# Where a query norm is multiplied in, and which engine forms the gate products, in a local-attention kernel on one core

## The chip, the cores and the metric

One Trainium2 chip, one core. The metric is the device time of one execution in microseconds, lower is better. The kernel before takes 1637.84 us, the median of three runs (1637.82 to 1640.18).

## The reference, cut to what matters

The input `x` is 16 sequences of 512 tokens with 128 features. The result is `x + _L0_attn_ref(xn) + _L0_ffn_ref(xn)` with `xn` the layer norm of `x`. The first is an attention among the 16 heads of each token, the second two layers of a local-attention block (`_layer`). The change touches only the layers, 16 sequences times 2 layers, called 32 units below. Per unit:

```python
q, k, v = to_heads(q), to_heads(k), to_heads(v)     # 8 heads of 64
q = l2norm(q) * qs
k = l2norm(k) * ksc
q, k = rotary_xpos(q, k)
sim = einsum('bhwid,bhwjd->bhwij', bq * QK_SCALE, bk)   # windows of 64, each sees itself and the one before
attn = softmax(where(mask, -max, sim))
...
h = layernorm(shift_token(x)) @ w1 + b1
a, g = split(h, 2)                                   # 341 wide each
x = x + (a * gelu(g)) @ w2 + b2
```

The rotation is linear, so the division by the norm of q may come before it, after it, or as a factor of the scores: softmax(rn * s) needs rn * s and the maximum times rn.

## The kernel before

**Units and blocks.** A unit (sequence s, layer l) has four blocks of 128 tokens. Every piece of work is a step (kind, s, l, n); a table gives each kind a slot (`UNIT_SLOTS` and the like, lines 50 to 95), `all_steps` (L123) adds the unit's place times `PERIOD` and sorts all steps by that number. Each engine's program walks this one sorted list and issues its own kinds in that order, so the slots alone set the order of every queue: TensorE, VectorE, ScalarE, GpSimd, and SyncE, which issues all transfers of the loop. The slots are no times; only their order acts. Semaphores (`Signal`, L171) make each step wait for what it reads and for the buffer that it overwrites. Five PSUM banks go round as a ring (`Ring`, L199): whichever is released earliest in the list is taken next, and `released_by` (L190) names the step that gives a bank back.

**One unit, as far as it matters here.** Per block: TensorE projects q and k (`project_qk`), ScalarE squares them (`square`, L621), VectorE multiplies by the rotary tables (`rope`, L808 and L813) and sums the squares (`ssq`, L823). GpSimd adds the two rotary parts over 1024 columns (`rope_add`, L554), and for two blocks at a time works out 1/norm of all 16 heads in twelve small operations (`rnorm`, L562, its lines in `newton` L515 to L530), into `rn`. Its step `normed` (L567) multiplies **k alone**, 512 columns, by its norm. TensorE transposes q and k (`qk_t`, L947), ScalarE copies them out of PSUM (`q_copy`, `k_copy`, line 597 as all plain copies), TensorE forms scores for the block as two half-blocks of four heads, one PSUM bank each (`scores`, L955 the mask and L961). VectorE takes the negated row maxima (`row_max`, L828, into `nmx`), and **GpSimd multiplies them by the norm of q** (`row_scale`, L577, into `nml`). ScalarE takes the exponentials, four ACTIVATEs of 128 columns per half-block, each followed by a read of its accumulator (`exp`, L644):

```python
nc.scalar.activation(pl[:, k, m, :], ps[:, m * P:(m + 1) * P], ACT.Exp, bias=nml[:, k, m:m + 1],
                     scale=rn[:, TURN[step] // 2 % RNS, 2 * m + n % 2:2 * m + n % 2 + 1], accum_out=suml[:, k, m:m + 1])
```

Both `bias` and `scale` are operands with one value per partition, called pointer operands here. That is 32 exponentials per unit, 1024 in all. VectorE forms the reciprocals of the sums (`row_recip`, L833). The probabilities are multiplied by them (`scale`): of the eight half-blocks of a unit, `POOL_SCALED = (1, 4, 6)` are done by GpSimd in one operation of 512 columns (L582), the other five by ScalarE in four of 128 (L651). Then come transposes (`probs_t`, L972), copies (`p_copy`), the products with v (`values`, L983; v was moved by transfers of SyncE, `move_v`, L474), a projection (`out_local`), a residual sum, a layer norm (`norm2`, L667), and the MLP.

**The MLP's gate.** For each of three column tiles (128, 128 and 85 rows of 512 columns) TensorE fills two banks (`up`). ScalarE takes the gelu of one into `gate` (`gelu`, L679, two buffers) and copies the other with its bias into `hid` (`up_copy`, L684). GpSimd multiplies the two (`hid`, L572), and `down` (L1024) waits for the third. ScalarE loads a function table before the first gelu of a unit and another before the next exponential.

Beside the units, the attention among heads (`_L0_attn_ref`) of each sequence runs on GpSimd (`product`, L549, 4.6 us each) and VectorE (L773, L784, L789, 2.3 us each), in single instructions that nothing can interrupt.

Of the kernel before, what the change touches and what calls it, by code (L numbers as in the profile page):

```python
# [13 lines left out]
P = 128  # L14
# [7 lines left out]
HT = 3  # L22
# [8 lines left out]
POOL_SCALED = (1, 4, 6)  # L31
# [10 lines left out]
FIRST_AT = (-1.2708745, 0.6010711, 2.0036151, 3.0013583, 4.0029550)  # L42
LAST_AT = (-5.0039757, -2.9663610, -1.9718764, -0.5737843, 0.4163776)
FIRST_HEADS = (0, 1, 2)
LAST_HEADS = (B - 2, B - 1)
HEADS_AT = (0.3413570, 0.4991559, 3.8117712, -4.4646283, -0.4851747)
HEADS_SCALE = (0.5958681, 1.1193597, 0.7838495, 1.0049087, 1.0274403)
# [9 lines left out]
    "k_copy": (165.0988, 171.4118, 184.9169, 201.8379), "scores": (170.7924, 176.2910, 190.1140, 206.8248),  # L57
    "row_max": (171.0266, 177.1326, 191.8920, 208.8231), "row_scale": (174.5908, 177.7892, 192.9950, 210.0411),
    "exp": (175.3308, 177.3865, 180.4114, 180.8920, 197.7475, 202.1735, 211.3702, 214.1910),
    "row_recip": (176.4316, 179.0744, 180.6813, 185.4614, 201.2478, 206.9631, 215.6879, 217.2619),  # L60
    "scale": (178.1679, 183.5201, 183.8322, 190.7280, 204.5029, 208.7350, 217.6800, 218.5197),
    "probs_t": (186.1063, 189.5048, 192.4912, 194.5274, 207.2222, 216.5516, 221.8074, 222.0460),
    "p_copy": (189.4922, 191.8301, 194.7040, 195.6005, 209.2029, 217.9046, 221.8298, 222.6642),
    "values": (196.4822, 199.5495, 223.8159, 224.0189), "o_copy": (199.8882, 201.3287, 225.0351, 226.7589),
    "out_local": (227.5112,), "x2": (230.4382,), "shift_x2": (233.0435,), "stats2": (235.6252,), "aggr2": (236.6378,),
    "rstd2": (237.6456,), "norm2": (242.9309,), "norm2_t": (244.3596,), "high2": (245.4327,), "low2": (245.7646,),
# [3 lines left out]
FIRST_SLOTS = {  # L70
    "shift_x": (117.3139,), "x1": (269.0942,), "shift_x1": (276.6645,), "x1_t": (276.8388,), "x1_split": (278.5542,),
    "x1_low": (280.0510,),
}
IN_SLOTS = {
    "load": (-60.4848,), "stats": (-40.1689,), "aggr": (-36.5136,), "rstd1": (-20.2682,), "norm": (15.7589,),
    "norm_t": (53.5376,), "x_split": (55.0099,), "x_low": (57.5271,),
}
HEADS_SLOTS = {
    "qkv_full": (78.2153, 89.6956, 104.7573, 110.3161), "qkv_bias": (81.5013, 91.1173, 108.0542, 113.9984),
    "product": (94.5851, 118.2468, 144.2400, 170.3617), "full_scores": (107.8015, 126.3480, 156.7184, 181.3058),  # L80
    "full_max": (109.2799, 132.3223, 160.4979, 185.2952), "full_less": (110.6705, 133.8879, 161.9904, 186.5792),
    "full_exp": (113.5148, 136.6825, 163.8463, 191.2888), "full_values": (116.5251, 143.0822, 166.7757, 194.4942),
    "full_out": (118.8605, 148.3945, 172.8347, 204.0966), "full_norm": (124.1554, 151.7265, 176.7351, 207.5981),
    "heads": (152.8697, 167.4103, 214.8847, 227.9640),
}
OUT_SLOTS = {
    "heads_load": (226.2026,), "attn_t": (237.0812,), "o_t": (241.2655,),
}
PREP_SLOTS = {
    "split_w3": (-91.8590,), "split_q": (65.5914, 68.6233), "tables": (61.3455, 105.5114), "fold": (145.8522,),  # L90
    "gain": (161.8664,), "split_up": (179.3697,), "biases": (148.4283,),
}
LAST_SLOTS = {
    "x_again": (236.0293,), "result": (270.2713,), "add_x": (270.8445,), "store": (329.0087,),
# [128 lines left out]
def build(nc, t, out):  # L223
    with ExitStack() as ctx:
# [43 lines left out]
        nmx = sb("nmx", [P, 4, 4])  # L268
# [85 lines left out]
        s_nml = signal("row_maxima_scaled", "row_scale")  # L354
# [21 lines left out]
        s_hid = signal("hidden", "hid")  # L376
        s_down = signal("down_filled", "down")
# [15 lines left out]
        def hidden_rows(n):  # L393
# [110 lines left out]
        def _(pool):  # L504
# [27 lines left out]
            for step in STEPS:  # L532
# [30 lines left out]
                if kind == "normed":  # L563
                    k3 = qk[:, TURN[step] % QKB, INNER:2 * INNER].rearrange("p (h d) -> p h d", d=LD)
                    pool.wait_ge(s_add.sem, s_add.at(same("rope_add", step, n), step))
                    pool.wait_ge(s_rn.sem, s_rn.at(same("rnorm", step, n // 2), step))
                    nc.gpsimd.tensor_tensor(k3, k3, rn[:, TURN[step] % RNS, LH:2 * LH, None].to_broadcast([P, LH, LD]), ALU.mult).then_inc(s_nrm.sem, 1)  # L567
                if kind == "hid":
                    pool.wait_ge(s_upc.sem, s_upc.at(same("up_copy", step, n), step))
                    pool.wait_ge(s_gelu.sem, s_gelu.at(same("gelu", step, n), step))  # L570
                    rows = hidden_rows(n)
                    nc.gpsimd.tensor_tensor(hid[rows, n, :], hid[rows, n, :], gate[rows, TURN[step] % 2, :], ALU.mult).then_inc(s_hid.sem, 1)  # L572
                if kind == "row_scale":
                    k = 2 * TURN[step] % PLS
                    pool.wait_ge(s_max.sem, s_max.at(same("row_max", step, n), step))
                    in_order(same("normed", step, n), step)
                    nc.gpsimd.tensor_tensor(nml[:, k:k + 2, :], nmx[:, 2 * TURN[step] % 4:2 * TURN[step] % 4 + 2, :],  # L577
# [513 lines left out]
```

## Time and profile before

| | |
|---|---|
| median of the runs | 1637.84 us |
| the profiled execution's own time | 1640.42 us |
| its span, from the first to the last instruction | 1638.6 us |
| mean granted TensorE clock | 0.969 of full speed |
| instructions | 40224 |
| function-table loads on ScalarE | 64 |

The profile is one execution. Busy time of an engine is the time covered by at least one of its instructions; ScalarE and GpSimd issue the next instruction before the last one's record has ended, so a mean duration is longer than what the instruction costs in a full queue. That cost is read from the distance between starts in the timeline.

### The profile page before, as it was taken

To read this page: it belongs to the slowest core of one execution; us is meant where nothing else is said; L and a number is where in the kernel's file an instruction comes from. 1 tells how busy PE (TensorE), PEld (TensorE's weight loads), DVE (VectorE), ACT (ScalarE), POOL (GpSimd) and SP (SyncE) were. 2 spreads that over 40 slices of the span, in tenths; PEclk is the share of its full clock that TensorE was granted. 3 is DMA by queue.
4 is the path that set the end of the run, shared out by engine and by line. 5 is a ranking of instruction groups with operands and counts; after the bars stand their busy time and mean duration, and the time that the engine had idled before them with its cause. 6 is when DMAs were issued, how large, how long until landed. Compare 5 with 4: busy or idle time off the path is not lost.

```text
span 1638.6 us, 40224 instructions
## 1 busy us (share of the span) xinstructions
PE 1384.8 (85%) x14680; PEld 1099.8 (67%) x14680; DVE 1342.5 (82%) x2149; ACT 1472.9 (90%) x4176; POOL 1237.4 (76%) x1607
## 2 busy tenths in 40 slices
PE   1578789998989989898989989998998988688885
PEld 1366577777777767777777767777777776577664
DVE  4998899898989989898888989898888686558731
ACT  1468799999999999999999999999999999598993
POOL 2758788787888888888888888788878784577741
PEclk9788899999999999999999999999999999899998
DMA  5021012221211122221211122121211211111120
GB/s 153 10 42 39 11 35 48 47 46 36 59 34 40 31 48 47 41 51 32 60 34 37 33 48 47 41 47 35 61 32 34 39 40 39 19 27 34 22 54 21
DMA packets 177637, 67.82 MB, mean 41 GB/s; under 512 B 146933, under 2 KB 152354, under 8 KB 177442
## 3 DMA queue, kind: packets, MB, share of 16 engines
q1 hardware_dynamic: 176146, 64.70, 18.7%
q8 instruction: 118, 1.93, 0.5%
q14 instruction: 77, 0.63, 0.1%
q10 hardware_dynamic: 1296, 0.56, 0.1%
HBM read 17.54 MB, written 8.39 MB: 16 GB/s over the span
## 4 chain that ended last, share of the span: by engine, by line
ACT 70%; PE 10%; issue 9%; DVE 5%; POOL 3%; DMA 1%; SPq 1%; ACTq 0%; DVEq 0%; POOLq 0%
ACT sb_pl L644 24%; ACT sb_pl L651 10%; ACT sb_pT L597 5%; ACT sb_sq L621 4%; ACT sb_kT L597 3%; ACT sb_oTl L597 3%; ACT sb_hid L684 3%; ACT sb_v L597 3%; ACT sb_hn L667 3%; ACT sb_qT L597 3%; PE banks L983 2%; ACT L679 2%; ACT L644 2%; ACT sb_gate L679 2%; PE banks L972 2%
## 5 line engine op out<-in xcount | busy, mean ns | idle before, releaser
L644 ACT ACTIVATE sb_pl<-banks,sb_nml,sb_rn 128x128 f32<-128x128 f32 x1024 | 466.0, 515 | 5.2 <-POOL sb_nml L577 4.8
L554 POOL TENSOR_TENSOR sb_qk<-sb_qk,sb_t 128x1024 f32<-128x1024 f32 x128 | 304.8, 2381 | 47.4 <-DVE sb_t L813 47.4
L549 POOL TENSOR_TENSOR sb_pr<-sb_qkvf 128x2048 f32<-128x2048 f32 x64 | 291.8, 4559 | 3.7 <-DVE sb_qkvf L767 3.7
L644 ACT ACTIVATION_READ_ACCUMULATOR sb_pl<-banks,sb_nml,sb_rn 128x1 f32 x1024 | 268.7, 262 | 0.0
L651 ACT ACTIVATE sb_pl<-sb_pl,sb_rl 128x128 f32<-128x128 f32 x640 | 213.1, 459 | 0.2 <-DVE sb_rl L833 0.2
L883 PE MATMUL banks<-sb_wqh,sb_hh 128*128 128x512 f32 x384 | 175.7, 458 | 43.6 <-DVE sb_t L813 34.5
L828 DVE TENSOR_REDUCE sb_nmx<-banks 128x4 f32<-128x512 f32 x256 | 164.1, 683 | 42.2 <-PE banks L961 42.1
L972 PE MATMUL banks<-sb_ident,sb_pl 128*128 128x128 f32 x1024 | 162.3, 283 | 27.7 <-ACT sb_kT L597 10.5
L621 ACT ACTIVATE sb_sq<-banks 128x1024 f32<-128x1024 f32 x128 | 137.3, 1073 | 44.1 <-PE banks L885 44.1
L597 ACT ACTIVATE sb_pT<-banks 128x512 f32<-128x512 f32 x256 | 165.8, 672 | 4.6 <-PE banks L972 4.5
L808 DVE TENSOR_TENSOR sb_qk<-banks,sb_tab 128x1024 f32<-128x1024 f32 x128 | 154.9, 1210 | 12.7 <-ACT sb_sq L621 12.6
L813 DVE TENSOR_TENSOR sb_t<-banks,sb_tab 128x512 f32<-128x512 f32 x256 | 163.5, 680 | 0.0
L572 POOL TENSOR_TENSOR sb_hid<-sb_hid,sb_gate 128x512 f32<-128x512 f32 (+1 forms) x96 | 122.5, 1285 | 53.9 <-ACT sb_hid L684 45.0
L972 PEld LDWEIGHTS banks<-sb_ident,sb_pl 128*128 128x128 f32 x1024 | 118.5, 143 | 64.1 <-issue 17.2
L947 PE MATMUL banks<-sb_ident,sb_qk 128*128 128x128 f32 x1024 | 146.3, 284 | 15.9 <-POOL sb_qk L567 11.7
L884 PE MATMUL banks<-sb_wql,sb_hh 128*128 128x512 f32 x384 | 157.5, 410 | 0.0
L885 PE MATMUL banks<-sb_wqh,sb_hl 128*128 128x512 f32 x384 | 157.5, 410 | 0.0
L823 DVE TENSOR_REDUCE sb_ssq<-sb_sq 128x16 f32<-128x1024 f32 x128 | 154.4, 1206 | 3.2 <-ACT sb_sq L621 3.2
L784 DVE TENSOR_TENSOR sb_pr<-banks,sb_qkvf 128x2048 f32<-128x2048 f32 x64 | 146.1, 2282 | 2.2
L961 PE MATMUL banks<-sb_kT,sb_qT 64*64 64x128 f32 x4096 | 144.5, 279 | 3.8 <-ACT sb_kT L597 3.8
L773 DVE TENSOR_REDUCE banks<-sb_pr 128x256 f32<-128x2048 f32 x64 | 145.8, 2279 | 0.0
L789 DVE TENSOR_REDUCE banks<-sb_pr 128x128 f32<-128x2048 f32 x64 | 145.6, 2275 | 0.0
(120 smaller groups left out, 3698.2 us busy)
## 6 DMA issues: line engine op xcount, KB each, us to landing
sb_vs<-sb_v SPq DMA_DIRECT2D x224, 128.0 KB, 2.4
sb_xt<-x SPq DMA_DIRECT2D x16, 256.0 KB, 3.0
heads_scratch<-sb_ofs SPq DMA_DIRECT2D x64, 64.0 KB, 3.3
sb_orow<-heads_scratch SPq DMA_DIRECT2D x16, 256.0 KB, 2.9
sb_ob<-x SPq DMA_DIRECT2D x16, 256.0 KB, 2.9
out<-sb_ob SPq DMA_DIRECT2D x16, 256.0 KB, 3.4
sb_hh<-sb_sh SPq DMA_DIRECT2D x16, 128.0 KB, 2.4
sb_hl<-sb_sl SPq DMA_DIRECT2D x16, 128.0 KB, 2.4
```

What stands on the lines that cost most here:

```text
L549: nc.gpsimd.tensor_tensor(pr[:].rearrange("p (q k d) -> p q k d", q=H, k=H), q[:, :, None, :].to_broadcast([P, H, H, D]), k[:, None, :, :] ...
L554: nc.gpsimd.tensor_tensor(qk[:, k, :], qk[:, k, :], t2[:, TURN[step] % 2, :], ALU.add).then_inc(s_add.sem, 1)
L597: return nc.scalar.activation(dst, src, ACT.Copy)
L621: nc.scalar.activation(sq[:, TURN[step] % 2, :], qk_ps, ACT.Square).then_inc(s_sq.sem, 1)
L644: last = nc.scalar.activation(pl[:, k, m, :], ps[:, m * P:(m + 1) * P], ACT.Exp, bias=nml[:, k, m:m + 1], scale=rn[:, TURN[step] // 2 % RN ...
L651: last = nc.scalar.activation(pl[:, k, m, :], pl[:, k, m, :], ACT.Copy, scale=rl[:, k, m:m + 1])
L813: last = nc.vector.tensor_tensor(t4[:, :, :, dst], q4[:, :, :, src], tab[:, l, n, 1, :, None, src].to_broadcast([P, 2, LH, 32]), ALU.mult)
L828: nc.vector.tensor_reduce(nmx[:, k + h, :], bank(same("scores", step, n), h).rearrange("p (a b) -> p a b", a=4), AX_X, ALU.max, negate=Tru ...
L883: mm(dst, ah, bh, start=True, stop=False)
L884: mm(dst, ah, bl, start=False, stop=False)
L885: return mm(dst, al, bh, start=False, stop=True)
L972: last = nc.tensor.transpose(ps[:, k * P:(k + 1) * P], pl[:, TURN[step] % PLS, k, :], ident[:])
```

## The change

It does five things.

1. `normed` on GpSimd multiplies q and k, 1024 columns, by their norms. The exponentials no longer have a `scale` operand and keep `bias`. `row_scale` is gone (128 operations); VectorE writes the negated maxima into `nml` itself, and `exp` waits for the maximum of its own half-block instead of the scaled maxima of both.
2. `POOL_HID = 1`: the first two gate products of a unit move to VectorE as one `scalar_tensor_tensor` that reads the PSUM bank, adds the bias and multiplies by the gate. Their two `up_copy` steps on ScalarE are gone. The third tile keeps `up_copy` and its product on GpSimd (`pool_hid`). `down` waits for both.
3. The banks of the first two tiles are released by `hid` on VectorE, no longer by `up_copy`. `gelu` waits for the product two before it, on whichever engine.
4. `POOL_SCALED = (2, 6)`: half-blocks 1 and 4 go to ScalarE and 2 to GpSimd, so ScalarE scales six and GpSimd two.
5. All slots are new, so every queue has a new order. The number of steps of other kinds is unchanged.

```diff
-POOL_SCALED = (1, 4, 6)
+POOL_HID = 1
+POOL_SCALED = (2, 6)
...
-    "normed": (154.4511, 162.8918, 182.9419, 183.7601), "project_v": (159.0725, 181.4664, 186.1013, 186.6209),
+    "normed": (182.3337, 183.2623, 200.1915, 201.2225), "project_v": (200.5275, 202.4083, 204.4952, 210.4119),
-    "v_copy": (159.9898, 183.8122, 188.2271, 189.9351), "move_v": (168.5510, 184.9583, 202.4625, 215.3760),
+    "v_copy": (201.3236, 202.6291, 210.9356, 212.3257), "move_v": (209.6570, 215.0451, 216.1022, 229.2302),
-    "qk_t": (161.6890, 171.0966, 184.0998, 201.0989), "q_copy": (164.6524, 171.1983, 185.3925, 201.7627),
+    "qk_t": (187.2993, 188.4284, 207.6851, 212.1740), "q_copy": (187.3831, 189.7285, 211.3468, 213.2392),
-    "values": (196.4822, 199.5495, 223.8159, 224.0189), "o_copy": (199.8882, 201.3287, 225.0351, 226.7589),
+    "values": (220.1959, 226.6013, 244.7089, 245.8630), "o_copy": (222.9003, 228.4260, 245.1633, 246.9817),
-    "up": (252.0156, 253.3813, 259.6720), "gelu": (252.2978, 256.7997, 260.5403), "up_copy": (253.6282, 256.7797, 260.7344),
-    "hid": (255.5584, 258.3963, 261.1113), "down": (266.3925,),
+    "up": (270.6924, 273.5245, 275.3137), "gelu": (273.1911, 273.8595, 275.4467), "up_copy": (276.3338,),
+    "hid": (275.1511, 275.2248), "pool_hid": (281.9469,), "down": (285.2914,),
...
-            "up": ("gelu", "up_copy")[k], "down": ("x1", "add_x")[l], "attn_t": "o_t"}[kind]
+            "up": ("gelu", "hid" if n < HT - POOL_HID else "up_copy")[k], "down": ("x1", "add_x")[l], "attn_t": "o_t"}[kind]
+    if last == "up_copy":
+        n -= HT - POOL_HID
...
+        def gated(step):
+
+            part = step[3] - (HT - POOL_HID)
+            return (s_hid, same("hid", step, step[3])) if part < 0 else (s_phid, same("pool_hid", step, part))
...
                 if kind == "normed":
-                    k3 = qk[:, TURN[step] % QKB, INNER:2 * INNER].rearrange("p (h d) -> p h d", d=LD)
+                    both = qk[:, TURN[step] % QKB, :].rearrange("p (h d) -> p h d", d=LD)
...
-                    nc.gpsimd.tensor_tensor(k3, k3, rn[:, TURN[step] % RNS, LH:2 * LH, None].to_broadcast([P, LH, LD]), ALU.mult).then_inc(s_nrm.sem, 1)
-                if kind == "hid":
+                    nc.gpsimd.tensor_tensor(both, both, rn[:, TURN[step] % RNS, :, None].to_broadcast([P, 2 * LH, LD]), ALU.mult).then_inc(s_nrm.sem, 1)
+                if kind == "pool_hid":
...
-                if kind == "row_scale":
...
-                    act.wait_ge(s_nml.sem, s_nml.at(same("row_scale", step, n // 2), step))
+                    act.wait_ge(s_max.sem, s_max.at(same("row_max", step, n // 2), step, n % 2 + 1))
...
                         last = nc.scalar.activation(pl[:, k, m, :], ps[:, m * P:(m + 1) * P], ACT.Exp, bias=nml[:, k, m:m + 1],
-                                                    scale=rn[:, TURN[step] // 2 % RNS, 2 * m + n % 2:2 * m + n % 2 + 1], accum_out=suml[:, k, m:m + 1])
+                                                    accum_out=suml[:, k, m:m + 1])
...
                     if before(step, 2):
-                        act.wait_ge(s_hid.sem, s_hid.at(("hid", *before(step, 2)[1:]), step))
+                        done, last = gated(before(step, 2))
+                        act.wait_ge(done.sem, done.at(last, step))
...
+                if kind == "hid":
+                    dve.wait_ge(s_up.sem, s_up.at(same("up", step, n), step, 2))
+                    dve.wait_ge(s_gelu.sem, s_gelu.at(same("gelu", step, n), step))
+                    rows, gates = hidden_rows(n), gate[hidden_rows(n), TURN[same("gelu", step, n)] % 2, :]
+                    nc.vector.scalar_tensor_tensor(hid[rows, n, :], bank(same("up", step, n), 1)[rows, :], b1[rows, l, 0, n:n + 1], gates,
+                                                   ALU.add, ALU.mult).then_inc(s_hid.sem, 1)
...
-                    pe.wait_ge(s_hid.sem, s_hid.at(same("hid", step, HT - 1), step))
+                    pe.wait_ge(s_hid.sem, s_hid.at(same("hid", step, HT - POOL_HID - 1), step))
+                    pe.wait_ge(s_phid.sem, s_phid.at(same("pool_hid", step, POOL_HID - 1), step))
```

## Rows read from the trace of the kernel before

**Rows 1.** The page, part 1: busy us (share of the span) xinstructions of each engine.

```profile
PE 1384.8 (85%) x14680; PEld 1099.8 (67%) x14680; DVE 1342.5 (82%) x2149; ACT 1472.9 (90%) x4176; POOL 1237.4 (76%) x1607
```

**Rows 2.** Busy time by stretch: length, PE, PEld, DVE, ACT, POOL, granted clock, DMA share, GB/s.

```profile
200.00:300.00 100.00, 88.58 (x931) 71.35 (x932) 91.63 (x147) 96.51 (x280) 83.98 (x103) 0.97 0.19 39
300.00:1300.00 1000.00, 909.56 (x9901) 721.00 (x9900) 887.18 (x1430) 990.35 (x2816) 832.01 (x1079) 1.00 0.21 43
1300.00:1639.00 339.00, 267.90 (x2815) 214.77 (x2815) 203.75 (x335) 277.11 (x780) 198.74 (x274) 0.94 0.14 31
```

**Rows 3.** Busy time by stretch, ACT's instructions of line 644 alone.

```profile
300.00:1300.00 1000.00, 356.62 (x1398) 1.00 0.21 43
```

**Rows 4.** Timeline of ACT, 700 to 748 us: start us, us, engine line op, shapes xcount.

```profile
702.53 0.46 ACT L644 ACTIVATE sb_pl<-banks,sb_nml,sb_rn 128x128 f32<-128x128 f32 x1
702.87 0.20 ACT L644 ACTIVATION_READ_ACCUMULATOR sb_pl<-banks,sb_nml,sb_rn 128x1 f32 x1
702.97 0.46 ACT L644 ACTIVATE sb_pl<-banks,sb_nml,sb_rn 128x128 f32<-128x128 f32 x1
...
712.11 1.35 ACT L651 ACTIVATE sb_pl<-sb_pl,sb_rl 128x128 f32<-128x128 f32 x4
713.28 1.09 ACT L621 ACTIVATE sb_sq<-banks 128x1024 f32<-128x1024 f32 x1
714.19 0.67 ACT L597 ACTIVATE sb_kT<-banks 128x512 f32<-128x512 f32 x1
714.66 0.68 ACT L597 ACTIVATE sb_qT<-banks 128x512 f32<-128x512 f32 x1
...
719.00 1.76 ACT L667 ACTIVATE sb_hn<-sb_x,sb_nmr,sb_rs 128x128 f32<-128x128 f32 x4
720.53 1.14 ACT L621 ACTIVATE sb_sq<-banks 128x1024 f32<-128x1024 f32 x1
...
728.62 1.28 ACT L679 ACT_TABLE_LOAD   x1
...
730.51 1.26 ACT L684 ACTIVATE sb_hid<-banks,sb_b 128x512 f32<-128x512 f32 x2
731.65 0.70 ACT L679 ACTIVATE sb_gate<-banks,sb_b 128x512 f32<-128x512 f32 x1
```

**Rows 5.** Groups by line and shape, ACT: xcount | busy us, mean ns | idle before.

```profile
L644 ACT ACTIVATE sb_pl<-banks,sb_nml,sb_rn 128x128 f32<-128x128 f32 x1024 | 466.0, 515 | 5.2 <-POOL sb_nml L577 4.8
L684 ACT ACTIVATE sb_hid<-banks,sb_b 128x512 f32<-128x512 f32 x64 | 42.4, 687 | 2.0 <-PE banks L885 2.0
```

**Rows 6.** The same view, POOL.

```profile
L554 POOL TENSOR_TENSOR sb_qk<-sb_qk,sb_t 128x1024 f32<-128x1024 f32 x128 | 304.8, 2381 | 47.4 <-DVE sb_t L813 47.4
...
L567 POOL TENSOR_TENSOR sb_qk<-sb_qk,sb_rn 128x512 f32<-128x512 f32 x128 | 133.8, 1046 | 4.4 <-issue 0.2
L582 POOL TENSOR_TENSOR sb_pl<-sb_pl,sb_rl 128x512 f32<-128x512 f32 x96 | 100.0, 1042 | 18.7 <-DVE sb_rl L833 18.7
L572 POOL TENSOR_TENSOR sb_hid<-sb_hid,sb_gate 128x512 f32<-128x512 f32 x64 | 81.5, 1284 | 38.9 <-ACT sb_hid L684 31.1 <-ACT sb_gate L679 7.8
...
L577 POOL TENSOR_TENSOR sb_nml<-sb_nmx,sb_rn 128x8 f32<-128x8 f32 x128 | 26.4, 207 | 59.6 <-DVE sb_nmx L828 59.4
```

**Rows 7.** The same view, DVE.

```profile
L857 DVE TENSOR_TENSOR sb_ml<-banks,sb_mh 128x512 fp32r<-128x512 f32 x32 | 22.1, 690 | 21.0 <-ACT sb_mh L597 20.8
```

**Rows 8.** Waits: engine, tile, line <- releaser: us in total, times, longest us.

```profile
DVE sb_rl L833 <- ACT sb_pl L644: 114.2, 103, 5.5
...
POOL sb_hid L572 <- ACT sb_hid L684: 45.0, 43, 8.1
...
POOL sb_hid L572 <- ACT sb_gate L679: 7.8, 14, 1.3
```

**Rows 9.** Waits of SyncE's own queue.

```profile
SPq L474 <- ACT sb_v L597: 452.8, 94, 26.1
```

**Rows 10.** The page, part 6: issues of transfers, KB each, us to landing.

```profile
sb_vs<-sb_v SPq DMA_DIRECT2D x224, 128.0 KB, 2.4
```

More of the change, by code:

```diff
@@ new lines @@
+    "k_copy": (188.2736, 192.0604, 211.5250, 213.9970), "scores": (191.0638, 195.0615, 213.0631, 225.7847),
+    "row_max": (191.4764, 195.6861, 216.0966, 226.7308),
+    "exp": (194.8833, 195.1833, 198.4961, 199.0827, 217.7930, 219.3748, 232.3456, 234.6785),
+    "row_recip": (195.2384, 196.7062, 202.6297, 203.8389, 222.8514, 225.3115, 237.9346, 238.1178),
+    "scale": (198.4786, 200.7005, 204.5438, 205.6352, 225.1242, 227.7413, 240.0089, 241.5326),
+    "probs_t": (201.3321, 205.9735, 214.4449, 214.6785, 228.5205, 239.9675, 241.9608, 243.5301),
@@ L69 @@
+    "hid": (275.1511, 275.2248), "pool_hid": (281.9469,), "down": (285.2914,),
 }
 FIRST_SLOTS = {
-    "shift_x": (117.3139,), "x1": (269.0942,), "shift_x1": (276.6645,), "x1_t": (276.8388,), "x1_split": (278.5542,),
-    "x1_low": (280.0510,),
+    "shift_x": (140.0838,), "x1": (286.1484,), "shift_x1": (286.2087,), "x1_t": (292.8402,), "x1_split": (294.2011,),
+    "x1_low": (294.7821,),
 }
 IN_SLOTS = {
-    "load": (-60.4848,), "stats": (-40.1689,), "aggr": (-36.5136,), "rstd1": (-20.2682,), "norm": (15.7589,),
@@ L76 @@
-    "norm_t": (53.5376,), "x_split": (55.0099,), "x_low": (57.5271,),
+    "load": (-43.2744,), "stats": (-42.8030,), "aggr": (-36.2465,), "rstd1": (-6.3194,), "norm": (27.1315,),
+    "norm_t": (75.6752,), "x_split": (77.7525,), "x_low": (79.2937,),
 }
 HEADS_SLOTS = {
-    "qkv_full": (78.2153, 89.6956, 104.7573, 110.3161), "qkv_bias": (81.5013, 91.1173, 108.0542, 113.9984),
-    "product": (94.5851, 118.2468, 144.2400, 170.3617), "full_scores": (107.8015, 126.3480, 156.7184, 181.3058),
-    "full_max": (109.2799, 132.3223, 160.4979, 185.2952), "full_less": (110.6705, 133.8879, 161.9904, 186.5792),
@@ L563, in _ @@
                 if kind == "normed":
-                    k3 = qk[:, TURN[step] % QKB, INNER:2 * INNER].rearrange("p (h d) -> p h d", d=LD)
+                    both = qk[:, TURN[step] % QKB, :].rearrange("p (h d) -> p h d", d=LD)
                     pool.wait_ge(s_add.sem, s_add.at(same("rope_add", step, n), step))
                     pool.wait_ge(s_rn.sem, s_rn.at(same("rnorm", step, n // 2), step))
-                    nc.gpsimd.tensor_tensor(k3, k3, rn[:, TURN[step] % RNS, LH:2 * LH, None].to_broadcast([P, LH, LD]), ALU.mult).then_inc(s_nrm.sem, 1)
-                if kind == "hid":
+                    nc.gpsimd.tensor_tensor(both, both, rn[:, TURN[step] % RNS, :, None].to_broadcast([P, 2 * LH, LD]), ALU.mult).then_inc(s_nrm.sem, 1)
+                if kind == "pool_hid":
+                    part = HT - POOL_HID + n
                     pool.wait_ge(s_upc.sem, s_upc.at(same("up_copy", step, n), step))
-                    pool.wait_ge(s_gelu.sem, s_gelu.at(same("gelu", step, n), step))
-                    rows = hidden_rows(n)
-                    nc.gpsimd.tensor_tensor(hid[rows, n, :], hid[rows, n, :], gate[rows, TURN[step] % 2, :], ALU.mult).then_inc(s_hid.sem, 1)
-                if kind == "row_scale":
[L574 to L577, printed above, removed]
-                                            rn[:, TURN[step] % RNS, 0:LH].rearrange("p (a h) -> p h a", h=2), ALU.mult).then_inc(s_nml.sem, 1)
+                    pool.wait_ge(s_gelu.sem, s_gelu.at(same("gelu", step, part), step))
+                    rows = hidden_rows(part)
+                    gates = gate[rows, TURN[same("gelu", step, part)] % 2, :]
+                    nc.gpsimd.tensor_tensor(hid[rows, part, :], hid[rows, part, :], gates, ALU.mult).then_inc(s_phid.sem, 1)
                 if kind == "scale" and n in POOL_SCALED:
@@ L680, in _ @@
                 if kind == "up_copy":
-                    act.wait_ge(s_up.sem, s_up.at(same("up", step, n), step, 2))
+                    part = HT - POOL_HID + n
+                    act.wait_ge(s_up.sem, s_up.at(same("up", step, part), step, 2))
                     in_order(same("gelu", step, 0), step)
-                    rows = hidden_rows(n)
-                    nc.scalar.activation(hid[rows, n, :], bank(same("up", step, n), 1)[rows, :], ACT.Identity, bias=b1[rows, l, 0, n:n + 1]).then_inc(s_upc.sem, 1)
+                    rows = hidden_rows(part)
+                    nc.scalar.activation(hid[rows, part, :], bank(same("up", step, part), 1)[rows, :], ACT.Identity, bias=b1[rows, l, 0, part:part + 1]).then_inc(s_upc.sem, 1)
                 if kind == "x1_split":
@@ L819, in _ @@
                     if old:
-                        in_order(same("row_recip", old, 2 * old[3] + 1), step)
+                        in_order(same("row_max", old, old[3]), step)
                         dve.wait_ge(s_rn.sem, s_rn.at(same("rnorm", old, old[3] // 2), step, 1))
```

52 lines of the change are left out of this document (24 added, 28 removed).

## The prediction

> **What bounds the kernel now.** I read the page's shares first: ScalarE is busy 90% of the span, TensorE 85%, VectorE 82% [rows 1]. That is an average, so the busy time by stretch comes next [rows 2]. From 300 to 1300 us, ScalarE is busy 990 of 1000 us, TensorE 910, VectorE 887, GpSimd 832. What limits this stage is ScalarE, and the others wait for it: VectorE's reciprocals wait 114.2 us in all for exponentials [rows 8]. ScalarE itself waits almost never; for the maxima that GpSimd scaled, 4.8 us in all [rows 5].
>
> How long is one unit there? Line 644 has 1398 instructions in that stretch [rows 3]; some 22 are table loads, one per unit, and a unit has 64 others (32 exponentials, 32 accumulator reads), so 1376/64 = 21.5 units, **46.5 us each**. Divided by 21.5, the busy times of a unit are ScalarE 46.1, TensorE 42.3, VectorE 41.3, GpSimd 38.7. ScalarE has 0.4 us of air, the next engine 4.2. TensorE's figure includes matmuls that overlap or wait with modelled ends, so its work is at most that.
>
> **ScalarE, term by term.** Its records overlap, so I price by distances between starts [rows 4].
> - *The scale operand.* A plain copy of 512 columns from PSUM has no pointer operand: 714.19 to 714.66, 0.47 us. The copy with a bias, same shape: 730.51 to 731.65 for two, 0.57 each. One pointer costs 0.10. From SBUF, four scalings with one pointer take 712.11 to 713.28, 0.2925 each; four norms with two pointers 719.00 to 720.53, 0.3825 each: 0.09. An exponential runs 702.53 to its accumulator read at 702.87, and 0.10 later the next one starts, 0.44 in all. I take **0.093 us** for the operand that goes, so 32 x 0.093 = 2.98 us less per unit, 95 us in the run. Bounds: 0.10 above; nothing below, if the read of the accumulator sets the distance. Against the low end: 0.47 less 384 columns at the rate that the square shows (1024 columns in 714.19 - 713.28 = 0.91, so 0.44 for 512 more, 0.33 for 384) leaves 0.14 for 128 columns without pointers; two pointers make 0.33, and 0.34 is seen. The operands explain the whole distance.
> - *Two bias copies fewer*: 2 x 0.57 = -1.14. *One more half-block to scale*: 4 x 0.2925 = +1.17. Together nothing. The third copy stays, and the order still has one block of gelus per unit between exponentials, so 64 table loads as before.
> - Sum: 46.1 - 2.95 = **43.1 us per unit**.
>
> **VectorE.** The gate product reads one PSUM bank and one SBUF tile of 512 columns; the nearest row is such an operation at 0.69 us [rows 7]. Two per unit: +1.38, so 41.3 becomes **42.7**. The added per-partition bias has no row on this engine; below, nothing; above, a second pass, 1.38 for each and 44.1 per unit. I take 0.69, since on ScalarE a pointer costs 0.1 and not a pass. `row_max` writes to another tile, at no cost.
>
> **GpSimd.** `normed` doubles from 512 columns at 1.046 us. Two full inputs go from 1.284 at 512 (line 572) to 2.381 at 1024 (line 554), so 0.19 is fixed; 2 x 1.046 - 0.19 = 1.90. I take 1.90 and keep 2.38 as the upper bound, that of two full inputs: +3.4 (at most +5.3) for four blocks. Gone are four `row_scale` (4 x 0.207), two gate products (2 x 1.284) and one scaling (1.042), 4.4 together [rows 6]. Net -1.0 (at most +0.9): 37.7 to 39.6 per unit, the slackest engine still. The row's 1.90 is 1.86 ns per column. The Trainium skill, GPSIMD Engine Reference, section 3.1, gives about 2.6 cycles an element for two inputs and 4497 ns for 2048, and says to do such products on VectorE; by an estimate from it, 1024 columns take 2.2 us, `normed` adds 4.8 us a unit, and GpSimd comes to 39.1. It advises against this part of the change; by its price, too, GpSimd would not bind.
>
> **The moved waits.** `exp` now waits for VectorE directly. GpSimd stood 59.4 us before `row_scale` [rows 6], a wait with `rope_add` and the long product queued behind it, which goes; what is late next there is the rotary product of VectorE (47.4 us before line 554 [rows 6]). New is a wait on VectorE: `hid` waits for `up` and a gelu, with rotary products and maxima queued behind it. GpSimd waited 45.0 + 7.8 us for the copies and gelus before 96 products [rows 8], 0.55 each; on VectorE that is 1.1 us per unit. It also holds the `up` bank until VectorE gets there, and a VectorE instruction of 2.3 us can be in front. The q norm now lies before `qk_t`, but the k norm already did and needed the same twelve steps; what is added is 0.86 us per block, and the new order does blocks in pairs, so the first transposes of a pair come up to 1.9 + 2.4 us later. In the loop earlier work covers that; without that cover, in the first and the last unit, it would cost some 4 us each.
>
> **Transfers.** None is added. In SyncE's queue `move_v` moves behind later copies of v; it waited 452.8 us in all for them [rows 9], and lands 2.4 us after issue [rows 10]. In the new order it still stands ahead of the `values` that read it by several steps of each engine. I cost it at nothing; if a landing were exposed, TensorE would stand 2.4 us.
>
> **Sum.** Now ScalarE needs 43.1, VectorE 42.7, TensorE at most 42.3. A ScalarE with 0.4 us of air needs the others to be idle 4 us a unit, which they no longer are. From 200 to 300 us, with VectorE at 92%, ScalarE was busy 96.5% [rows 2]: 3.5% of 43.1 is 1.5 us of air. Between 0.4 and 1.5 I take 1.2: **44.3 us per unit**, 2.2 less. Over 21.5 units that is 47 us. The other 10.5 units hold 10.5 x 2.98 = 31 us of the saving; ScalarE is busy 277 of the last 339 us [rows 2] and the start hangs on other engines, so I take 13. In all -60, from the profiled execution's 1640.4 to 1580.4; that execution is 2.6 above the median of the runs, so **1578 us**.
>
> **The rivals.**
> - *All of it arrives* (0.13). ScalarE keeps its 0.4 us: 1637.8 - 94 = 1544, to 1560 with a weaker start. For it: ScalarE hardly waits for anything now. Against: three engines within 1 us.
> - *VectorE becomes the bound* (0.14). It stood 114.2/32 = 3.6 us per unit before the reciprocals [rows 8]. If 1.5 to 2.7 of this stays beside 1.1 of new waits, a unit takes 42.7 + 2.6 to 3.8 = 45.3 to 46.5, and little is left: 1605 to 1634.
> - *The operand is free* (0.08): the accumulator read sets the distance. Then ScalarE stays at 46.1 and VectorE is fuller: 1636 to 1650, half of it within 0.2%. Against it stands the sum of pointers above.
> - *Slower by the gate products* (0.07): VectorE stands at `hid` behind a table load (1.28 us) and a gelu (0.70) [rows 4] with the exponentials ahead. It decides at 46.5 - 42.7 = 3.8 us of new standing per unit, 1.9 for each product. At 2.5 each, a unit takes 47.7: 1.2 x 32 = 38 us more, **1676**. For it: both products are queued together right behind the first gelus. Against it: the 0.55 seen on GpSimd.
> - *The forecast* (0.58): 1562 to 1605.
>
> **The numbers.** A measurement of this kernel tells some 0.2%, 3.3 us, from no change. Faster: 0.58 + 0.13 + 0.14 = 0.85. Same: half the free operand and the edge of VectorE's case, 0.05. Slower: 0.10. The range holds the forecast's own and parts of the two on either side, 1550 to 1618; 2 in 10 stay outside.
>
> **What would show it.** In the profile after: exponential to accumulator read 0.25 instead of 0.34, and 0.35 from one exponential to the next; on ScalarE 64 bias copies fewer and 128 scalings more; `normed` near 1.9 us; the gate product near 0.69 on VectorE; VectorE near 95% busy in the middle, ScalarE 96 to 98%, units 44.3 us apart. The forecast is wrong if the exponential's distance stays, if `hid` on VectorE waits more than 2 us a unit, or if `normed` takes over 2.4.

## The result and the profile after

The changed kernel takes **1541.68 us** (median of 4 runs, 1538.84 to 1544.04) against 1638.24 for the kernel before, ratio 0.9408 with the interval 0.9385 to 0.943. That is 97 us less where I forecast 60, and 8 us below the range. The profiled execution took 1544.04 us, its span is 1542.3.

The page of the changed kernel, part 1, answers to [rows 1]; below it, busy time by stretch answers to [rows 2], in the same columns.

```profile
PE 1355.6 (88%) x14680; PEld 1105.4 (72%) x14680; DVE 1365.6 (89%) x2213; ACT 1378.2 (89%) x4240; POOL 1209.4 (78%) x1383
```

```profile
200.00:300.00 100.00, 89.75 (x941) 72.89 (x940) 89.70 (x142) 93.28 (x289) 82.25 (x87) 0.97 0.20 42
300.00:1300.00 1000.00, 945.48 (x10614) 775.46 (x10613) 958.51 (x1571) 990.09 (x3065) 866.15 (x991) 1.00 0.22 46
```

ScalarE's busy time fell by 94.7 us (1472.9 to 1378.2). In the middle VectorE is busy 959 us of 1000, near the 95% that I had listed; ScalarE is busy 990, as before, where I had listed 96 to 98%.

The operand, in the timeline of ScalarE in the changed kernel (start us, us, engine line op, shapes):

```profile
710.23 0.36 ACT L647 ACTIVATE sb_pl<-banks,sb_nml 128x128 f32<-128x128 f32 x1
710.49 0.20 ACT L647 ACTIVATION_READ_ACCUMULATOR sb_pl<-banks,sb_nml 128x1 f32 x1
710.58 0.37 ACT L647 ACTIVATE sb_pl<-banks,sb_nml 128x128 f32<-128x128 f32 x1
```

From the exponential to its accumulator read 0.26 us, to the next exponential 0.35, where [rows 4] show 0.34 and 0.44: 0.09 us less. The Trainium skill, ScalarE: Activation LUTs, section What ACT_TABLE_LOAD costs, says that each per-partition pointer operand adds about 93 ns; the trace agrees, also for an exponential with an accumulator (0.09 us).

How long a unit is can be read without counting, from the first instruction of the unit's layer norm (`norm2`, L667 before, L670 after; one start per unit). These are those of the fifth and the 27th unit in the timeline of ScalarE, first of the kernel before, then of the changed one.

```profile
349.13 0.62 ACT L667 ACTIVATE sb_hn<-sb_x,sb_nmr,sb_rs 128x128 f32<-128x128 f32 x1
...
1365.76 0.61 ACT L667 ACTIVATE sb_hn<-sb_x,sb_nmr,sb_rs 128x128 f32<-128x128 f32 x1
```

```profile
346.45 0.70 ACT L670 ACTIVATE sb_hn<-sb_x,sb_nmr,sb_rs 128x128 f32<-128x128 f32 x1
...
1295.07 0.69 ACT L670 ACTIVATE sb_hn<-sb_x,sb_nmr,sb_rs 128x128 f32<-128x128 f32 x1
```

Before: 1016.6/22 = 46.21 us per unit. After: 948.6/22 = **43.12**. So 68 us came from these 22 units, 3 from the start (349.1 to 346.5), and 26 from what lies behind the 27th start (1638.6 - 1365.8 = 272.8 against 247.2). This split, start, unit and end, is used for all runs below.

The stretches between these two starts hold 22 whole units, so busy time divided by 22 is free of cut units. First the kernel before, then the changed one, in the columns of [rows 2]:

```profile
349.13:1365.76 1016.63, 923.22 (x10070) 732.01 (x10068) 895.31 (x1443) 1006.04 (x2870) 840.08 (x1095) 1.00 0.20 42
```

```profile
346.45:1295.07 948.62, 897.76 (x10065) 736.71 (x10061) 909.54 (x1487) 940.10 (x2913) 821.12 (x941) 1.00 0.21 45
```

ScalarE is busy 45.7 us per unit before and 42.7 after, and idle 0.5 and 0.4; VectorE is busy 40.7 and 41.3.

The groups by line and shape of the changed kernel give the other prices (count | busy us, mean ns | idle before).

```profile
L574 POOL TENSOR_TENSOR sb_qk<-sb_qk,sb_rn 128x1024 f32<-128x1024 f32 x128 | 241.2, 1906 | 0.6
L867 DVE SCALAR_TENSOR_TENSOR sb_hid<-banks,sb_b,sb_gate 128x512 f32<-128x512 f32 x64 | 45.2, 746 | 14.9 <-ACT sb_gate L683 9.6 <-PE banks L896 5.3
L838 DVE RECIPROCAL sb_rl<-sb_suml 128x4 f32<-128x4 f32 x256 | 37.8, 166 | 15.5 <-ACT sb_pl L647 14.9
```

`normed` takes 1.906 us, where I took 1.90 (by my estimate from the Trainium skill, GPSIMD Engine Reference, section 3.1, it was 2.2; the measurement decides). The gate product takes 0.71 us by its busy time (45.2/64), where I took 0.69, and VectorE waits 14.9 us in all before them, 0.47 per unit and not 1.1. The wait that could have made VectorE the bound is gone: 114.2 us before the reciprocals [rows 8] became 14.9. Their group in the kernel before:

```profile
L833 DVE RECIPROCAL sb_rl<-sb_suml 128x4 f32<-128x4 f32 x256 | 42.2, 166 | 114.6 <-ACT sb_pl L644 114.2
```

### The profile page after: what moved, and what is told of

The parts are those of the page before. It is cut to its first block, busy times and chain, and to the rows that moved or that the text cites. A ratio compares the mean times of both kernels' runs of the same rounds, so it can differ in the third digit from the quotient of the medians.

```text
span 1542.3 us, 40144 instructions
## 1 busy us (share of the span) xinstructions
PE 1355.6 (88%) x14680; PEld 1105.4 (72%) x14680; DVE 1365.6 (89%) x2213; ACT 1378.2 (89%) x4240; POOL 1209.4 (78%) x1383
## 4 chain that ended last, share of the span: by engine, by line
ACT 54%; DVE 19%; PE 12%; issue 6%; DMA 5%; SPq 2%; POOL 1%; POOLq 0%; ACTq 0%; DVEq 0%
ACT sb_pl L647 16%; ACT sb_pl L654 9%; ACT sb_pT L600 4%; ACT sb_gate L683 3%; ACT sb_sq L624 3%; DMA sb_xt<-x 3%; DVE sb_t L818 3%; DVE banks L794 3%; DMA sb_x<-sb_x 2%; DVE sb_pr L789 2%; DVE banks L778 2%; DVE sb_nml L833 2%; ACT sb_oTl L600 2%; DVE sb_qk L813 2%; ACT L647 2%
## 5 line engine op out<-in xcount | busy, mean ns | idle before, releaser
L647 ACT ACTIVATE sb_pl<-banks,sb_nml 128x128 f32<-128x128 f32 x1024 | 369.3, 429 | 15.3 <-DVE sb_nml L833 14.8
L647 ACT ACTIVATION_READ_ACCUMULATOR sb_pl<-banks,sb_nml 128x1 f32 x1024 | 270.4, 269 | 0.0
L654 ACT ACTIVATE sb_pl<-sb_pl,sb_rl 128x128 f32<-128x128 f32 x768 | 259.8, 480 | 0.3 <-DVE sb_rl L838 0.2
L574 POOL TENSOR_TENSOR sb_qk<-sb_qk,sb_rn 128x1024 f32<-128x1024 f32 x128 | 241.2, 1906 | 0.6
L833 DVE TENSOR_REDUCE sb_nml<-banks 128x4 f32<-128x512 f32 x256 | 163.9, 683 | 18.5 <-PE banks L972 18.5
L624 ACT ACTIVATE sb_sq<-banks 128x1024 f32<-128x1024 f32 x128 | 142.1, 1110 | 37.5 <-PE banks L896 37.4
L983 PE MATMUL banks<-sb_ident,sb_pl 128*128 128x128 f32 x1024 | 155.9, 284 | 20.9 <-ACT sb_pl L654 16.9
L958 PE MATMUL banks<-sb_ident,sb_qk 128*128 128x128 f32 x1024 | 140.0, 281 | 16.4 <-ACT sb_pT L600 9.9
L972 PEld LDWEIGHTS banks<-sb_kT,sb_qT 64*64 64x64 f32 x4096 | 111.4, 133 | 49.7 <-issue 45.1
```

The costliest lines, as they stand in the source:

```text
L574: nc.gpsimd.tensor_tensor(both, both, rn[:, TURN[step] % RNS, :, None].to_broadcast([P, 2 * LH, LD]), ALU.mult).then_inc(s_nrm.sem, 1)
L624: nc.scalar.activation(sq[:, TURN[step] % 2, :], qk_ps, ACT.Square).then_inc(s_sq.sem, 1)
L647: last = nc.scalar.activation(pl[:, k, m, :], ps[:, m * P:(m + 1) * P], ACT.Exp, bias=nml[:, k, m:m + 1], accum_out=suml[:, k, m:m + 1])
L654: last = nc.scalar.activation(pl[:, k, m, :], pl[:, k, m, :], ACT.Copy, scale=rl[:, k, m:m + 1])
L833: nc.vector.tensor_reduce(nml[:, k + h, :], bank(same("scores", step, n), h).rearrange("p (a b) -> p a b", a=4), AX_X, ALU.max, negate=Tru ...
L983: last = nc.tensor.transpose(ps[:, k * P:(k + 1) * P], pl[:, TURN[step] % PLS, k, :], ident[:])
```

## The experiments

Each ratio is to the kernel before, run on the same chip, with its 95% interval. "Against the changed kernel" is the difference of the ratios times 1638 us; the changed kernel itself came out at 0.941 on a second chip (d4).

| run | ratio | against the changed kernel | start, unit, end (us) |
|---|---|---|---|
| kernel before | 1 | +97 | 349, 46.21, 273 |
| changed kernel | 0.9408 (0.9385 to 0.943) | 0 | 346, 43.12, 247 |
| a8 norm alone, old order | 0.9646 (0.9632 to 0.966) | +39 | 347, 44.11, 264 |
| a2 all operations, old order | 0.9657 (0.9643 to 0.9672) | +41 | 345, 44.15, 268 |
| a1 operand back | 0.9871 (0.9853 to 0.9889) | +76 | 356, 45.63, 263 |
| a4 gates back | 0.9684 (0.967 to 0.9699) | +45 | 349, 44.24, 264 |
| a5 VectorE, two more | 0.9516 (0.9501 to 0.953) | +18 | 345, 43.66, 252 |
| a6 ScalarE, two more | 0.9532 (0.9516 to 0.9547) | +20 | 350, 43.74, 250 |
| b1 old order, new last places | 0.9717 (0.9702 to 0.9731) | +51 | 344, 44.10, 278 |
| b2 new order, old last places | 0.9615 (0.9601 to 0.9629) | +34 | 345, 43.17, 280 |
| c1 old order, o_copy moved | 0.9784 (0.977 to 0.9799) | +62 | 345, 44.77, 274 |
| c3 new order, o_copy back | 0.9471 (0.9457 to 0.9486) | +10 | 344, 43.52, 250 |
| a7 third half-block on GpSimd | 0.9378 (0.9359 to 0.9397) | -5 | 347, 42.50, 249 |
| a3 order alone | 1.1509 (1.1481 to 1.1538) | +344 | 394, 54.75, 290 |
| d1, d2 out_local moved | 1.0825, 1.0821 | +232 | 367, 51.3, 276 |

**Is the operand the whole saving?** (a1)

```diff
-                                                    accum_out=suml[:, k, m:m + 1])
+                                                    scale=one[:, m:m + 1], accum_out=suml[:, k, m:m + 1])
```

> The changed kernel, but every exponential has a scale operand again, one value per partition from a tile of ones; order, queues and all other work stay those of the changed kernel. Theory A (the operand is the whole saving: ScalarE's queue sets the time and 0.093 us in each of 1024 exponentials arrives in full): 1542 + 95 = 1637 us, 1630 to 1642. Theory B (my forecast's arithmetic was right on the operand, some 60 us, and the new order gave the other 36): 1542 + 60 = 1602, and under 1620. Exponential to accumulator read 0.34 us in both.

Measured: +76 us, 1620.67 in its own runs. That lies between the two theories' 95 and 60; scaled to the changed kernel's chip it is 1617 us, just inside theory B's bound of 1620. The unit grew by 2.51 of the 2.98 us that were put back. The distance from exponential to read is back at 0.35 (702.02 to 702.37 in its timeline). With the operand in place, the change's order and its other parts still save 21 us.

**The norm part alone, and all operations, in the old order** (a8, a2). The slot tables are those of the kernel before; a8 also keeps three gate products and half-blocks 1, 4 and 6 on GpSimd.

```diff
-POOL_HID = 1
-POOL_SCALED = (2, 6)
+POOL_HID = 3
+POOL_SCALED = (1, 4, 6)
```

> Part 1 alone, in the old order: normed over q and k, no scale operand, no scaling of maxima; all three gate products and half-blocks 1, 4 and 6 stay on GpSimd, whose work rises by 3.4 - 0.8 = 2.6 us per unit to 41.3 by its busy time. Theory A: ScalarE's sum is again 43.1 per unit, and GpSimd's 41.3 overstates its work, so 1542 to 1560 us. Theory B (engines within 2 us of each other disturb one another): 1578 to 1600. If parts 2 and 4 of the change were needed to relieve GpSimd, this run is over 1580.

> The changed kernel's operations in the old order: the slot tables of the kernel before, with the two VectorE products where the first two products stood and the third copy and product where the third stood. Theory A: the order matters little, 1542 to 1555 us. Theory B: without the new order the saving is the 60 of the forecast, 1578, and at least 1565.

Measured: 0.9646 and 0.9657, 58 and 56 us less than before. Theory A falls, theory B holds: **without the new order the saving is nearly the 60 us that I forecast**, and the unit takes 44.11 and 44.15 us where I forecast 44.3. In the old order, parts 2 and 4 bring nothing (a2 against a8, the intervals overlap): GpSimd's load in a8, 928 of 1000 us busy in the middle, is carried as it is. (a8 is just over the 1580 us that was to mean that it is not; a2, where the load is gone, is no faster.) The new order brings 41 us, a2 against the changed kernel: 1.03 us in each of 22 units and 21 us at the end.

```profile
300.00:1300.00 1000.00, 922.83 (x10358) 756.24 (x10358) 917.72 (x1488) 976.26 (x2946) 927.67 (x1038) 1.00 0.21 44
```

This is a8's middle, in the columns of [rows 2]: ScalarE 976 of 1000 us, against 990 in both kernels. The same 22 whole units of a2, and then of a8:

```profile
344.80:1316.10 971.30, 893.87 (x10072) 736.60 (x10070) 915.40 (x1489) 950.36 (x2914) 823.90 (x942) 1.00 0.21 44
```

```profile
346.70:1317.00 970.30, 895.65 (x10068) 733.27 (x10066) 888.54 (x1444) 947.89 (x2870) 899.32 (x1008) 1.00 0.21 44
```

ScalarE is idle 0.95 and 1.02 us per unit there, close to the 1.2 of air that I had put in the sum, and 0.39 in the new order. Of the 1.03 us per unit between a2 and the changed kernel that is 0.56; the other 0.47 is in ScalarE's busy records (43.20 against 42.73), for the same operations.

**The order alone, in the old code** (a3).

> The kernel before with nothing but the new slot tables (scaling of maxima right behind each maximum, bias copies right behind their gelus; GpSimd scales half-blocks 1, 4 and 6 as before). Theory A: 1638 us within 10 us, since ScalarE's work is that of before. Theory B: 1600 to 1620.

Measured: 1.1509, which neither theory allows, and the run doesn't tell them apart. I had put the scaling of the maxima right behind each maximum, and in the new order that is a bad place in GpSimd's queue. The waits of a3 between 300 and 1300 us:

```profile
POOL sb_nml L577 <- DVE sb_nmx L828: 193.3, 61, 7.5
```

GpSimd stood 193 us for maxima, with everything behind it, where it stood 59.4 in the whole run before [rows 6]. The run also differs from the changed kernel by the operand and the bias copies, which cost 76 and 45 us by themselves (a1, a4), and its granted clock in that stretch was 0.92, where it was 1.00 before. So the 344 us are not the price of one wait, and what the new order does with the old code stays open. What the run suggests about the change is that `row_scale` ties GpSimd's queue to TensorE and VectorE, and that the change takes that tie away; no run shows what this is worth.

**How near are the other engines?** (a5, a6, a4). One more VectorE product in front of each gate product, or one more copy of ScalarE in front of `q_copy` 0 and 2, into a tile that nobody reads:

```diff
+                    nc.vector.tensor_tensor(spill[rows, :], bank(same("up", step, n), 1)[rows, :], gates, ALU.mult).then_inc(s_spill.sem, 1)
```

> The changed kernel with each VectorE gate product preceded by one more product of the same two inputs into a tile that nobody reads: 64 more instructions, about 0.6 us each in a full queue, 1.2 us per unit. If VectorE has the 1 to 2 us of air that lies between 41.3 busy and 43.1 per unit: under +10 us. If the engines are so close that each sets the time in turn (the idea behind my 1.2 us of air): +20 to +38. Ratio to before 0.945 against 0.955 to 0.964.

> The changed kernel with two more plain copies of 512 columns per unit on ScalarE, into a tile that nobody reads: 2 x 0.48 = 0.96 us per unit. If ScalarE's queue sets the time in full: +31 us, ratio to before 0.960. If it sets only part of it: +15 or less.

Measured: 1.2 us more work per unit on VectorE cost 18 us in all, 0.54 per unit; 0.96 us more on ScalarE cost 20, 0.62 per unit. VectorE's is below my 20 to 38 and over the 10 of the other case; ScalarE's is short of 31. It is also over the 15 of its other case. So added work on either passes on in part, about half and two thirds: the changed kernel does not follow one engine alone. ScalarE's idle time, read over 22 units as above, rose from 0.39 to 0.86 us per unit with the work on VectorE, and fell to 0.17 with the work on ScalarE (busy 42.80 of 43.66 us, and 43.57 of 43.74). Each kind of work was added in one place only, and the share may hang on the place.

> The changed kernel with part 2 undone: all three tiles are copied by ScalarE and multiplied by GpSimd, in the places where the change has its gelus and products. ScalarE gets 2 x 0.57 = 1.14 us more per unit, GpSimd 2.57 more, VectorE 1.4 less. Theory A' (ScalarE's queue sets the unit in this order): +36 us on the changed kernel, ratio to before 0.963. If waits of the copies on a GpSimd that is fuller count too: up to +60. If VectorE's products had cost the loop anything: less than +30.

Measured: +45 us, in the 36 to 60 that was expected. The unit grew by 1.12 us, about the two bias copies (2 x 0.57), and the end by 17 us. In the new order part 2 pays; GpSimd's two added products were not separated from the copies.

**One wait of the old order, taken out and put back** (c1, c3). In the kernel before, ScalarE's last copy of probabilities is followed by `o_copy` 2, which waits for TensorE's `values`. The waits of ScalarE between 300 and 1300 us, first of the kernel before, then of a2, then of the changed kernel:

```profile
ACT sb_oTl L597 <- PE banks L983: 7.9, 21, 0.4
```

```profile
ACT sb_oTl L600 <- PE banks L994: 8.9, 22, 0.4
```

```profile
ACT sb_pl L647 <- DVE sb_nml L833: 6.0, 11, 0.6
ACT sb_hn L670 <- POOL sb_nmr L595: 1.9, 5, 0.6
```

The first two are once per unit, 0.4 us each by the records, 0.54 by the distances between starts (a record's end overlaps the wait). The new order has exponentials of the next unit in between. c1 moves `o_copy` 2 and 3 so in the old order; c3 puts `o_copy` 2 back ahead of these exponentials in the new one. No other queue changes its order. But the ring of banks goes by the places too: by the kernels' own `Ring`, 102 of TensorE's 1425 bank fills follow another earlier user of their bank in c1 than in a2, and 67 in c3 than in the changed kernel, so TensorE's waits for banks can move as well. This was not separated from the move itself. The edit of c1:

```diff
-    "values": (196.4822, 199.5495, 223.8159, 224.0189), "o_copy": (199.8882, 201.3287, 225.0351, 226.7589),
+    "values": (196.4822, 199.5495, 223.8159, 224.0189), "o_copy": (199.8882, 201.3287, 225.3340, 227.3890),
```

> The kernel of a2_old_order with ScalarE's third and fourth copy of heads out of a unit (o_copy 2 and 3) moved behind the first and second group of four exponentials of the next unit, as the new order has them; every other queue is unchanged. In a2 ScalarE stands some 0.54 us per unit between its last copy of probabilities and o_copy 2, until TensorE has formed the values; in the changed kernel it does not. Theory E (the middle of the old order loses to such stands of ScalarE, one by one): the unit falls from 44.15 to 43.6 us, the time by 14 to 18 us, ratio to before 0.955 to 0.958. Theory F (the stands are symptoms of engines that are all full, and another wait takes its place): under 6 us, ratio 0.962 or more.

> The reverse: the changed kernel with o_copy 2 ahead of the next unit's first exponentials, every other queue unchanged. Theory E: +0.5 us per unit, 14 to 18 us, ratio 0.950 to 0.952. Theory F: under 6 us, ratio 0.944 or less.

Measured: c3 costs 10 us, 0.40 per unit, between the two theories; the wait is back (9.5 us, 23 times). c1 does not save 14 to 18 us; it costs 21, on theory F's side. The waits of c1 in the same stretch, of ScalarE and then of TensorE:

```profile
ACT sb_sq L624 <- PE banks L896: 16.5, 32, 1.0
ACT sb_v L600 <- PE banks L896: 8.4, 10, 0.8
```

```profile
PE banks L1004 <- ACT sb_oTl L600: 16.6, 22, 1.0
```

The wait before `o_copy` is gone from ScalarE. Now TensorE stands before `out_local` (L1004), 16.6 us where a2 has 1.7, since the last copy that it reads comes four exponentials later; and the next unit's projection stands behind it in TensorE's queue, so ScalarE waits for that at `square` (L624), 16.5 us where a2 has 0.2. Nearly the same move is worth 10 us in one order and costs 21 in the other. In the new order the projection stands ahead of `out_local`; that this is the reason is not shown.

**Moving the reader too** (d1, d2).

```diff
-    "out_local": (227.5112,), "x2": (230.4382,), "shift_x2": (233.0435,), "stats2": (235.6252,)
+    "out_local": (233.2800,), "x2": (233.5000,), "shift_x2": (233.6000,), "stats2": (235.6252,)
```

> The kernel of c1_old_order_o_copy (copies of heads out moved behind the next unit's first exponentials, 0.9784) with the step that reads them moved too: out_local stands behind the next unit's project_qk 0 on TensorE, with the residual sum and its shift behind it, as the new order has it; ScalarE's queue is that of c1. In c1 ScalarE no longer stands before o_copy 2 but TensorE stands before out_local, and square 0 waits 0.73 us per unit for the projection queued behind it. Theory G (a stand goes only if every queue that it touches is moved together): the unit falls from 44.77 to 43.5 to 44.0 us, ratio 0.952 to 0.962, below a2's 0.9657. Theory F (the engines are too full for it): a new wait takes its place, 0.9657 or more.

> The kernel of a2_old_order with out_local moved as in d1, and the copies of heads out left where they were. Theory G: within 0.5% of a2, ratio 0.961 to 0.970, since ScalarE still stands 0.54 us before o_copy 2. If the place of out_local alone is what counts: 0.960 or less.

Measured: 1.0825 and 1.0821, some 190 us over a2 and on theory F's side for d1, and the same with and without the move of `o_copy`. So the place of `out_local` was wrong in a way of its own: it came behind `project_qk` 0, which waits for VectorE's rotary products of an earlier block, and VectorE, with little moved in its own queue, waits for `out_local` in turn. Waits of d2 between 300 and 1300 us, of TensorE and of VectorE:

```profile
PE banks L894 <- DVE sb_t L818: 106.7, 50, 3.3
```

```profile
DVE sb_x L846 <- PE banks L1004: 93.9, 20, 6.1
DVE sb_st L851 <- DMA sb_x<-sb_x: 60.8, 20, 3.1
```

VectorE stood 4.7 us in each unit for `out_local`, where a2 has 0.1, and 3.0 for the transfer behind it, where a2 has 1.3. TensorE's standing has a second price here. In d2 it stood 2.9 us, up to 713.72, and the granted clock from 714 to 718 us was 0.57, where it was 1.00 from 710 to 714; the projection's matmuls of 512 columns then started 0.43 us apart instead of 0.23. Over the middle the clock was 0.93 in d1 and d2. How the loss divides between the waits and the clock was not measured. Theory G's numbers did not come; its idea stays open, since these moves brought waits of their own.

**The places of the last units** (b1, b2).

```diff
-LAST_AT = (-5.0039757, -2.9663610, -1.9718764, -0.5737843, 0.4163776)
+LAST_AT = (-4.9945847, -2.9959306, -1.9923118, -0.9899664, 0.0148815)
```

> The kernel of a2_old_order (the change's operations in the old order) with one table of places changed: the last five units stand where the changed kernel has them (LAST_AT; the last two units 1.00 periods apart and 0.4 to 0.6 periods earlier). a2 took 0.9657 of the kernel before, and behind its 27th unit it needed 268 us where the changed kernel needs 247. Theory C (the last units' places make that difference): about 20 us less than a2, ratio 0.953. Theory D (it comes from the order within the units, and the places fit only their own slots): within 8 us of a2 or slower, ratio 0.961 or more.

> The changed kernel with the places of the last five units as in the kernel before (LAST_AT; the last two units 0.42 and 0.40 periods later). If these places gave the end its 21 us, as the gap of 58 instead of 40 us between the norms of two of the last units suggests: +15 to +22 us, ratio 0.950 to 0.954. If not: within 6 us.

Measured: in the new order the old places cost 34 us, more than expected; the end takes 280 us instead of 247. In the old order the new places don't save 20 us but cost 10 (end 278 instead of 268), as theory D had it. So the 21 us at the end belong to tables and places together. Beside the places, the old and the new tables differ at many steps, which were not tried one by one.

**A version that beats both** (a7, d3, d4).

```diff
-POOL_SCALED = (2, 6)
+POOL_SCALED = (2, 4, 6)
```

> The changed kernel with a third half-block (number 4) scaled on GpSimd instead of ScalarE: 4 x 0.2925 = 1.17 us less on ScalarE per unit, 1.04 more on GpSimd. If only ScalarE's queue set the time: -37 us, ratio 0.918. With VectorE as near as a5 says (0.45 us passed on per us added), its 41.3 us of work is the next bound: -10 to -20 us. If the wait for GpSimd, behind its long instructions, reaches the transposes: slower than the changed kernel.

> The kernel of a7_three_on_pool once more, beside the changed kernel on the same chip and in five rounds. Its unit took 42.50 us against 43.12, 22 x 0.62 = 14 us less in the middle; its intervals overlapped with those of the changed kernel. If it is really the faster: 4 to 12 us below d4.

> The changed kernel itself, as the measure for the others of this call: ratio 0.9385 to 0.943 again.

Measured: a7 took 5 us less than the changed kernel, with overlapping intervals, and short of the 10 to 20 that was expected. Side by side on one chip, d3 took 0.9368 (0.9354 to 0.9382) and d4 0.941 (0.9397 to 0.9423); medians 1535.72 and 1543.05 us. A third half-block on GpSimd is faster by 7 us, and the intervals are apart. So in the new order it cost time to take one half-block from GpSimd, as part 4 does; the old choice (1, 4, 6) was not run with the changed kernel's operations and order. 1.17 us less on ScalarE shortened the unit by 0.48 to 0.62. The middle of a7:

```profile
300.00:1300.00 1000.00, 954.05 (x10744) 788.34 (x10742) 964.06 (x1590) 979.14 (x3013) 890.36 (x1017) 1.00 0.22 46
```

ScalarE is busy 979 of 1000 us, VectorE 964, TensorE 954: the load is now spread, and less is to be had from ScalarE alone.

## Why the prediction was wrong

- **The operand's price was right.** 0.093 us forecast, 0.09 read; ScalarE's busy time fell by 94.7 us, where 32 units of 2.95 us give 94. The rival that the operand is free is refuted.
- **The unit before was taken too long.** I had counted records in a window that cuts units and got 46.5 us; the starts give 46.21. So ScalarE's work before was 45.7 us per unit, not 46.1, and my sum for the changed kernel should have read 45.7 - 2.95 = 42.8, not 43.1. It measured 42.7. That the changed unit of 43.12 us equals my sum of 43.1 is chance: it is 42.7 of work and 0.4 of air. The error cancels where the forecast takes differences of units.
- **GpSimd and VectorE were priced right, VectorE's sum was not.** 1.906 and 0.71 us against 1.90 and 0.69. But VectorE's busy time per unit, over the 22 whole units, is 909.5/22 = 41.3 us, not 42.7; before it was 895.3/22 = 40.7, not 41.3. The products added 2 x 0.71 = 1.4, and 0.8 vanished elsewhere. One place shows in the groups of VectorE. The same 256 reciprocals have records of 166 ns in both kernels, but add 42.2 us of busy time before and 37.8 after, when VectorE no longer waits in front of them. So records overlap their neighbours more in a fuller queue, and an engine that waits looks fuller than its work. I see this as the reason for the rest too, but traced only the reciprocals. The true room of VectorE was larger than my sum gave it.
- **The step that failed is the air of 1.2 us per unit**, and with it the 13 us for the rest of the run; behind both stands the new order, which I had costed at nothing. I wrote that "A ScalarE with 0.4 us of air needs the others to be idle 4 us a unit, which they no longer are". In the changed kernel ScalarE keeps its 0.4 us, with VectorE 96% busy; the unit fell by 3.09 us, not 2.2, and the rest of the run gave 28 us, not 13. a2 and a8 show what the step had right: with these operations in the old order the air is 0.95 and 1.02 us, the unit fell by 2.06 and 2.10, the rest gave 9 and 11 us, and the whole saving was 56 and 58 us where I said 60. Every edit to the order had been read only for what it might expose (transfers, transposes), not for what it might close. It is worth 41 us here. "All of it arrives" got 0.13 and was the case that came (2 us below even its own lower end), though not as I told it: there, too, the order stood for nothing.
- **Where the 41 us lie:** 23 in the middle. Of these the place of `o_copy` is worth 0.40 us per unit (c3), and that wait was nearly all of ScalarE's air before the change (7.9 of 9.7 idle us in the middle); the other 0.6 us per unit were not taken apart. 21 lie at the end, with the places of the last units, which work only with the tables that they were made for (b1, b2). The start is 2 us later.
- **The two causes don't add.** With the operand in place, everything else in the change saves 21 us (a1); without it the order alone saves 41 (a2). In the old order part 1 as a whole (the operand, `row_scale` and the longer `normed`) saves 58 us (a8), in the new one the operand by itself 76 (a1). The operand alone in the old order was not run. My reading, argued and not shown, is that ScalarE's time, once given back, is used fully only where the other queues are arranged to feed it sooner.
- **Slower by the gate products** did not come: VectorE waits 0.47 us per unit before them, not 3.8. The range failed since it ended at 1550, inside the case "all of it arrives" (1544 to 1560), to which I had given 0.13; its lower bound should have been the full sum, 1544, less what an order can close.

## What to carry to other kernels

Price an operand by the distance between starts of two forms that differ in it; a few rows gave 0.09 to 0.10 us here, and 0.09 came. Where a change also re-orders in-order queues by hand or by a planner, the order is a term of its own with a range on both sides: the same operations took 41 us more in the old order, and small moves out of a planned order cost 10 (c3, b1), 21 (c1), 34 (b2) and 191 us (d2 against a2). The busy time of an engine that often waits can overstate its work (here the reciprocals' 42.2 us against 37.8), so the room of the second engine can be larger than its share says.

## What was not expected of the hardware

The operand's 95 us of work on an engine that is 99% busy were worth 76 us in the new order, and the whole of part 1 no more than 58 in the old one. And work added where an engine is full passes only in part: 0.54 of 1.2 us on VectorE at 96%, 0.62 of 0.96 on ScalarE at 99%. A busy share of 99% did not mean that the time follows that engine one to one.
